# First attention layer: keys and values stored unsplit, dense products by pairs, and another order of TensorE's work in a slot

## The reference

```
q = einsum('bsh,he->bse', x, w_q).reshape(b, sq, GROUPS, HPG, KVC)      # 4 groups of 4 heads, 128 each
k, v = split(einsum('bsh,he->bse', x, w_kv), 2)                         # 4 groups of 128 each
scores = einsum('bqgpd,bkgd->bqgpk', q, k) * KVC ** -0.5
probs = softmax(where(causal, scores, -inf), axis=-1)
ctx = einsum('bqgpk,bkgd->bqgpd', probs, v).reshape(b, sq, HEADS * KVC)
return einsum('bse,eh->bsh', ctx, w_dense)
```

## Time and profile before

| | |
|---|---|
| runs, median | 3868.26 us |
| the profiled execution | 3867.56 us |
| its span, first to last instruction | 3865.7 us |
| TensorE busy, granted clock over the span | 89%, 0.947 |
| VectorE, ScalarE, GpSimd busy | 63%, 41%, 29% |
| stage `l0kv`, first product to the first instruction of `l0h` | 52.4 to 127.3 us |
| heads, first scores to last dense product | 139.4 to 1059 us |

### The profile page before, as it was taken

One profiled execution on the slowest core, in us unless ns is written; L12 is line 12 of the kernel. 1 busy time (PEld: TensorE's weight loads), 2 busy tenths in 40 slices (PEclk: granted clock), 3 DMA queues, 4 the chain that ended last, 5 costly groups with the idle time before them and its releaser, 6 DMA issues. The chain is left out here.

```text
span 3865.7 us, 65600 instructions
## 1 busy us (share of the span) xinstructions
PE 3422.4 (89%) x21360; PEld 2634.4 (68%) x21360; DVE 2453.4 (63%) x4610; ACT 1578.6 (41%) x2855; POOL 1106.9 (29%) x819
## 2 busy tenths in 40 slices
PE   6598998989869799999998669999859999699997
PEld 4477877777747588888886235555438888388883
DVE  4455555655532565666655578889468888388883
ACT  3344444544422444444443224666433333233332
POOL 1000000000013566666664320000013444444444
PEclk8799999999989899999999888999979999899998
DMA  4301000010010100000000232222034443134431
GB/s 144 133 3 45 3 23 24 3 46 1 1 34 0 48 17 18 18 18 18 18 16 0 76 122 80 82 80 83 30 104 115 114 114 97 35 107 114 114 97 48
DMA packets 146336, 216.75 MB, mean 56 GB/s; under 512 B 23824, under 2 KB 87184, under 8 KB 145936
## 3 DMA queue, kind: packets, MB, share of 16 engines
q1 hardware_dynamic: 140112, 207.33, 17.2%
q0 software_dynamic: 6144, 8.39, 1.3%
HBM read 170.45 MB, written 44.96 MB: 56 GB/s over the span
## 5 line engine op out<-in xcount | busy, mean ns | idle before, releaser
L1912 DVE TENSOR_REDUCE l2h_half<-l2h_s 128x1 f32<-128x512 f32 x512 | 337.5, 685 | 49.1 <-PE l2h_s L1814 48.1
L570 DVE TENSOR_REDUCE l0h_negtop<-l0h_sc 128x1 f32<-128x128 f32 (+7 forms) x256 | 192.9, 754 | 224.0 <-PE l0h_sc L485 221.4
L1899 ACT ACTIVATE l2h_PT<-l2h_s 128x1024 f32<-128x1024 f32 x256 | 248.3, 1022 | 163.9 <-PE l2h_s L1824 163.9
L642 ACT ACTIVATE l0h_PTH<-l0h_tp 128x512 fp32r<-128x512 f32 (+3 forms) x384 | 174.6, 488 | 254.8 <-PE l0h_tp L496 254.7
L559 POOL TENSOR_TENSOR l0h_wq_lo<-l0h_wq,l0h_wq_hi 128x256 fp32r<-128x256 f32 x16 | 11.8, 738 | 826.1 <-ACT l0h_wq_hi L628 826.1
L1814 PE MATMUL l2h_s<-l2h_K,l2h_Q 128*128 128x512 f32 x512 | 218.7, 466 | 23.3 <-DMA l2h_K<-l_split 20.8
L496 PE MATMUL l0h_tp<-ident,l0h_probs 128*128 128x128 f32 x1152 | 179.6, 279 | 63.0 <-DVE l0h_PTL L589 62.9
L652 ACT ACTIVATE l0h_probs<-l0h_sc,l0h_negtop 128x128 f32<-128x128 f32 (+7 forms) x256 | 190.3, 744 | 94.3 <-DVE l0h_negtop L570 93.4
L589 DVE TENSOR_TENSOR l0h_PTL<-l0h_tp,l0h_PTH 128x512 fp32r<-128x512 f32 (+3 forms) x384 | 200.8, 550 | 32.2 <-ACT l0h_PTH L642 29.2
L159 POOL TENSOR_TENSOR XN<-XN,n_rstd 128x512 f32<-128x512 f32 x32 | 39.8, 1266 | 594.2 <-DVE n_rstd L140 594.2
L511 PE MATMUL l0h_cx<-l0h_PTH,l0a_VH 128*128 128x256 f32 (+1 forms) x640 | 196.4, 307 | 0.0
(11 more groups left out here) (418 smaller groups left out, 9809.1 us busy)
## 6 DMA issues: line engine op xcount, KB each, us to landing
l3p_decb<-l_decays SPq DMA_DIRECT2D x128, 256.0 KB, 4.4
l3p_w<-L_w SPq DMA_DIRECT2D x34, 512.0 KB, 3.6
l2h_Q<-l_split SPq DMA_DIRECT2D x64, 256.0 KB
l2h_K<-l_split SPq DMA_DIRECT2D x64, 256.0 KB
l3p_prow<-l_decays SPq DMA_DIRECT2D x128, 128.0 KB, 3.1
l_split<-l2q_hi SPq DMA_DIRECT2D x16, 512.0 KB, 3.6
l_split<-l2q_lo SPq DMA_DIRECT2D x16, 512.0 KB, 3.8
l3p_wgu<-L_ffn_w_gate_up SPq DMA_DIRECT2D x32, 256.0 KB, 4.8
```

The lines of the kernel that those rows point to most:

```text
L570: dve.reduce_max(negtop[:, i % 4:i % 4 + 1], sc[s % 2][:, 0:(t + 1) * P], AX_X, negate=True).then_inc(top_ready, 1)
L642: act.activation(PTH[:, pair % 2, 4 * j:4 * j + m, i % 2 * P:(i % 2 + 1) * P], tp[n % 2][:, 0:m * P].rearrange("p (m n) -> p m n", m=m), A ...
L1899: act.activation(PT[:, b, kb, :], s2[kb % 2][:, :], ACT.Exp, scale=L2_SCALE).then_inc(exped, 1)
L1912: dve.reduce_max(half[:, b, t, z:z + 1], bank(slot_of(i))[:, :], AX_X).then_inc(s1_read, 1)
```

## The change

- Keys and values lie in DRAM as they come from the product, in one part. ScalarE and VectorE take every second job and copy it out, and there are eight staging buffers instead of four. Group 0 is loaded after job 23.
- A load goes into the low part's tile (`KL`, `VL`), and GpSimd splits it in place in two passes of 128x1024: the high part is the loaded number plus zero, rounded, and the low part is the difference. SP doesn't wait for landings any more; the semaphores that TensorE waits for come from GpSimd.
- The dense products of a pair are issued together, four slots after its second unit, into both halves of `outp`, and added together. Inverses of row sums are taken by twos.
- High and low queries are made in two halves of 512 columns, and VectorE makes the low queries after the low part of the turn of that slot.
- TensorE's order in a slot becomes: scores or projection, dense pair, values, turn.

```diff
@@ l0_kv @@
-                act.activation(hi[:, n % NB, :], acc[n % 8][:, :], ACT.Copy).then_inc(hi_ready, 1)
-                dve.tensor_tensor(lo[:, n % NB, :], acc[n % 8][:, :], hi[:, n % NB, :].bitcast(F32), ALU.subtract).then_inc(lo_ready, 1)
+                act.activation(raw[:, n % NB, :], acc[n % 8][:, :], ACT.Copy).then_inc(act_kept, 1)
+                dve.tensor_copy(raw[:, n % NB, :], acc[n % 8][:, :]).then_inc(dve_kept, 1)
...
+            def _(pool):
+                pool.wait_ge(zeroed, 1)
+                for b in range(B):
+                    split_keys(pool, kv, 0, b)
+                    split_values(pool, kv, 0, b)
@@ new @@
+def split_keys(pool, kv, g, b):
+    tok = slice(b * S, (b + 1) * S)
+    pool.wait_ge(kv.k_loaded[b], 16 * g + 16)
+    pool.tensor_tensor(kv.KH[:, tok], kv.KL[:, tok].bitcast(F32), kv.zero[:, :], ALU.add).then_inc(kv.k_rounded[b], 1)
+    pool.wait_ge(kv.k_rounded[b], g + 1)
+    pool.tensor_tensor(kv.KL[:, tok], kv.KL[:, tok].bitcast(F32), kv.KH[:, tok].bitcast(F32), ALU.subtract).then_inc(kv.keys_here[b], L0_HPG)
@@ l0_heads, SP and GpSimd: group(g, last) @@
...
-                        keys_arrived(g + 1, 0)
-                        values_arrived(g + 1, 0)
...
+                        for b in range(B):
+                            sp.wait_ge(scores_ready, NU * end + NQ * (b + 1))
+                            load_keys(sp, kd, kv, g + 1, b)
+                            sp.wait_ge(pv_done, NPAIR * end + NPAIR // B * (b + 1))
+                            load_values(sp, vd, kv, g + 1, b)
...
+                    for i in range(L0_HPG):
+                        h = L0_HPG * g + i
+                        if not last or i < L0_HPG - 1:
+                            split_weights(h + 1)
+                    if not last:
+                        for b in range(B):
+                            split_keys(pool, kv, g + 1, b)
+                            split_values(pool, kv, g + 1, b)
@@ l0_heads, TensorE @@
                 def dense(h, i):
-                    pe.wait_ge(ctx_ready, NPAIR * h + i // 2 + 1)
-                        pe.wait_ge(added, NU * h + i)
-                    pe.matmul(outp[:, 0:D], ctxT[:, i // 2 % 2, i % 2 * P:(i % 2 + 1) * P], wd[:, ds(h, 1), :].rearrange("p a n -> p (a n)"),
-                              start=True, stop=True).then_inc(dense_done, 1)
+                    pe.wait_ge(ctx_ready, NPAIR * h + pair + 1)
+                        pe.wait_ge(added, NPAIR * h + pair)
+                    for j in range(2):
+                        mm = pe.matmul(outp[:, j * D:(j + 1) * D], ctxT[:, pair % 2, j * P:(j + 1) * P],
+                                       wd[:, ds(h, 1), :].rearrange("p a n -> p (a n)"), start=True, stop=True)
+                    mm.then_inc(dense_done, 1)
                 def step(h, s):
-                    if u := unit_at(h, s, 2):
-                        turn_probs(*u)
-                    if u := unit_at(h, s, 5):
+                    if (u := unit_at(h, s, 4)) and u[1] % 2:
                         dense(*u)
                     if (u := unit_at(h, s, 3)) and u[1] % 2:
                         weigh_values(*u)
+                    if u := unit_at(h, s, 2):
+                        turn_probs(*u)
@@ l0_heads, VectorE: step @@
-                        elif exists(h + 1 - i):
-                            low_queries(2 * h + (3 if i == 0 else 2), i, sc[s % 2])
                     if u := unit_at(h, s, 2):
-                        invert(*u)
+                        if u[1] % 2:
+                            invert(*u)
                         low_probs(*u)
+                    if kind == "query" and exists(h) and exists(h + 1 - i):
+                        low_queries(2 * h + (3 if i == 0 else 2), i, sc[s % 2])
-                    if u := unit_at(h, s, 5):
+                    if (u := unit_at(h, s, 4)) and u[1] % 2:
                         add_dense(*u)
```

More of the change, by code:

```diff
@@ L275, in l0_kv, with kept @@
         FIRST = TT + NJ
[L277 to L285, removed]
+        def kept(engine, n):
+            engine.wait_ge(dve_kept if n % 2 else act_kept, n // 2 + 1)
         with nc.Block() as block:
@@ L290, in _ @@
             def _(sp):
[L291 to L295, removed]
+                for c in range(DC):
+                    sp.dma_start(wkv[:, c, :], rows(a["L0_attn_w_kv"])[:, c, :]).then_inc(w_loaded, 16)
+                for n, (kind, i, j) in enumerate(jobs):
+                    if n == FIRST + NB // 2:
+                        for m in range(NB):
+                            sp.wait_ge(stored[m], 16 * (FIRST // NB + (m < FIRST % NB)))
                         for b in range(B):
@@ L298, in _ @@
                             load_values(sp, vd, kv, 0, b)
[L299 to L304, removed]
+                    kept(sp, n)
+                    if kind == "k":
+                        sp.dma_start(kd[i][:, j * BANK:(j + 1) * BANK], raw[:, n % NB, :]).then_inc(stored[n % NB], 16)
+                    else:
+                        sp.dma_start(vd.rearrange("g p t n -> p t g n")[:, i], raw[:, n % NB, :].rearrange("p (g n) -> p g n", g=L0_GROUPS)).then_inc(stored[n % NB], 16)
+                for m in range(NB):
+                    sp.wait_ge(stored[m], 16 * (len(jobs) // NB))
             @block.tensor
@@ L322, in _ @@
             def _(act):
-                act.wait_ge(w_loaded, 16)
                 for c in range(DC):
+                    act.wait_ge(w_loaded, 16 * DC)
                     act.activation(w_hi[:, c, :], wkv[:, c, :], ACT.Copy).then_inc(whi_ready, 1)
-                for n in range(len(jobs)):
+                for n in range(0, len(jobs), 2):
                     act.wait_ge(made, n + 1)
-                    wait(act, stored[n % NB], 32 * (n // NB))
-                    act.activation(hi[:, n % NB, :], acc[n % 8][:, :], ACT.Copy).then_inc(hi_ready, 1)
+                    wait(act, stored[n % NB], 16 * (n // NB))
+                    act.activation(raw[:, n % NB, :], acc[n % 8][:, :], ACT.Copy).then_inc(act_kept, 1)
             @block.vector
             def _(dve):
+                dve.memset(kv.zero[:, :], 0.0).then_inc(zeroed, 1)
                 for c in range(DC):
@@ L335, in _ @@
                     dve.tensor_tensor(w_lo[:, c, :], wkv[:, c, :], w_hi[:, c, :].bitcast(F32), ALU.subtract).then_inc(wlo_ready, 1)
-                for n in range(len(jobs)):
-                    dve.wait_ge(hi_ready, n + 1)
-                    wait(dve, stored[n % NB], 32 * (n // NB))
-                    dve.tensor_tensor(lo[:, n % NB, :], acc[n % 8][:, :], hi[:, n % NB, :].bitcast(F32), ALU.subtract).then_inc(lo_ready, 1)
+                for n in range(1, len(jobs), 2):
+                    dve.wait_ge(made, n + 1)
+                    wait(dve, stored[n % NB], 16 * (n // NB))
+                    dve.tensor_copy(raw[:, n % NB, :], acc[n % 8][:, :]).then_inc(dve_kept, 1)
+            @block.gpsimd
+            def _(pool):
[3 more added lines that the diff above has]
+                    split_values(pool, kv, 0, b)
 def l0_heads(nc, k, a, kd, vd, kv):
@@ L545, in _ @@
                     j, c = divmod(n, DC)
[L546 removed]
+                    pe.wait_ge(added, NPAIR * L0_HEADS)
                     wait(pe, x_added, n - 3)
@@ L561, in _, with group @@
                 split_weights(0)
-                with pool.Fori(1, L0_HEADS) as h:
-                    split_weights(h)
+                def group(g, last):
+                    for i in range(L0_HPG):
[6 more added lines that the diff above has]
+                            split_values(pool, kv, g + 1, b)
+                with pool.Fori(0, L0_GROUPS - 1) as g:
+                    group(g, False)
+                group(L0_GROUPS - 1, True)
             @block.vector
@@ L626, in split_weights @@
                     act.wait_ge(wq_loaded, 16 * h + 16)
-                    wait(act, q_made, 2 * h)
+                    wait(act, q_made, 4 * h)
                     act.activation(wq_hi[:, :, :], wq[:, :, :], ACT.Copy).then_inc(whi_ready, 1)
                 def high_queries(n, b, bank):
-                    act.wait_ge(q_made, n)
-                    act.activation(QH[:, b * S:(b + 1) * S], bank[:, :], ACT.Copy, scale=L0_SCALE).then_inc(qh_ready, 1)
+                    for j in range(S // BANK):
+                        act.wait_ge(q_made, 2 * n - 1 + j)
+                        act.activation(QH[:, b * S + j * BANK:b * S + (j + 1) * BANK], bank[:, j * BANK:(j + 1) * BANK], ACT.Copy,
+                                       scale=L0_SCALE).then_inc(qh_ready, 1)
                 def high_probs(h, i):
```

94 lines of the change are left out of this document (44 added, 50 removed).

## The result

| | before | after |
|---|---|---|
| runs, median (us) | 3865.11 (3860.75 to 3872.4) | 3939.86 (3932.48 to 3944.92) |
| span of the profiled execution | 3865.7 | 3943.1 |
| first scores of the heads | 139.4 | 124.4 |
| heads, first scores to last dense product | 919.6 | 1012.8 |

The change makes the kernel slower: the ratio is 1.019 (95%: 1.0164 to 1.0216). The heads take 93.2 us more and begin 15.1 sooner, which makes 78, and the span has 77.4.

A forecast was written before the change was run, and what follows sets the result against it. TensorE was taken to bound the heads, working nearly all the time but waiting for VectorE's low parts and adds. 3867.6 + 96 (heads, with 12 of low clock) - 12 (first stage) = 3951, said as 3950; range 3875 to 3995.

The forecast's parts named there:

- New waits: TensorE in the heads: values wait for low parts, dense pairs for the context copy; 6.45 us a half head with refilling.
- t0: Slot of a half head: values of t2/t3 wait for the low part, with only t0's scores as cover; 1.6 us.
- t2: Slot of a half head: dense pair waits for the copy behind high parts and two half queries; 1.6 us.
- t3: Slot of a half head: values of t6/t7 wait for the first low tile; 1.0 us.
- t1: Slot of a half head: dense pair waits for the copy behind high parts and t0's exponential; 1.1 us.
- t7: Slot of a half head: dense pair waits for the copy behind high parts and t6's exponential; 0.4 us.
- t6: Slot of a half head: values of t4/t5 wait for the low part; 0.35 us.
- W: TensorE's work in one half head, unchanged by the change: 24.9 us, between 24.5 and 25.4.
- Low clock: Heads: time lost to TensorE's lower granted clock, taken as half of before's 14 stretches, 12 us.
- Waits are not hidden: Answers the rival that the heads' new waits are mostly hidden: faster, 3848 with half of 6.45 left; chance 0.10.
- the clock does not fall in every half: Answers the rival that the clock falls in every half head, costing 54 instead of 12: 3992; chance 0.12.
- nothing blocks VectorE: Answers the rival that GpSimd's passes block VectorE in the heads: up to 57 us more, 4007; chance 0.05.

The follow-up runs named there:

- order only: Kernel before with only TensorE's slot order changed (turn last, dense products still single): 4103.67 us, ratio 1.0603.
- Copy first: Kernel after with ScalarE's context copy moved to the front of its step, ahead of high parts and exponential: 3859.14 us, ratio 0.9965.
- values last: Kernel after with the values moved behind the turn on TensorE, the dense pair staying ahead of it: 3850.4 us, ratio 0.9957.
- turn first: Kernel after with TensorE's turn moved back ahead of the dense pair and the values: 3766.31 us, ratio 0.9732.
- unsplit only: Kernel before with only the unsplit keys and values (first stage, loads, GpSimd's splits): 3860.5 us, ratio 0.9973.
- low queries only: Kernel before with only VectorE's low queries moved behind the low part of that slot's turn: 3823.11 us, ratio 0.9887.

## Why the prediction was right

The forecast of 3950 came out 10 above the median, by its own mechanism.

- *Waits that go.* The turn's wait for low parts and the dense product's wait for adds vanish, as said. The single edits tell the two apart. For the turn's wait of 62.9 the moved order suffices ("order only" leaves 1.0), and so nearly do the late low queries (4.7 left). The wait for adds is taken by the pairs; the moved order alone raises it from 19.1 to 184.7.
- *New waits.* Values for low parts and dense pairs for the copy, longest in t0 and t2. With the 0.2 that the list leaves out, slot by slot: t2 1.6 (1.6 said), t3 1.0 (1.0), t0 1.6 (1.6), t1 1.14 (1.1), t7 0.36 (0.4), and t6, at 533.13 in the next half, 0.43 (0.35); together 6.1 (6.05). PE's idle time in the heads comes to 159.6 + 186 x 0.2 = 197 by the same reckoning (200 said). Copy first and values last take the two kinds apart.
- *Work.* W was 24.9; "turn first" has (838.7 - 2)/32 = 26.15 a half without low clock and two waits of together 1.18 listed and 0.2 unlisted each, so W is some 24.6. The half of after, (1012.8 - 27)/32 = 30.8, leaves 6.2 for new waits (6.45 said). Together they are 0.55 below the forecast of 31.35, which is 17 us less. The 0.07 for refilling the array behind each wait, 0.4 a half in the sum, is shown by no run: in the kernel after the first product of the values is followed by the second after 0.22 us behind a wait (484.16) and after 0.20 without one (502.10), 0.02 at that place.
- *Low clock.* 12 us were said, half of before's, as no wait would be longer than 1.85; one was, of 1.98 in the last half. Low clock cost 27, in 9 stretches instead of 14, seven of them twice as long. The profiled execution is the longest of four (3944.92), so the usual loss may be some us less. This step was mis-sized by 15 us and nearly cancels the 17: that the total came so close is in part luck. Here are 10 us of one in the kernel after (windows as in the earlier trace rows):

```profile
494.00:496.00 2.00, 2.00 (x14) 2.00 (x14) 0.00 (x0) 0.25 (x1) 0.00 (x0) 0.63 0.00 0
496.00:498.00 2.00, 1.42 (x6) 1.05 (x6) 1.29 (x4) 1.13 (x5) 0.00 (x0) 0.50 0.00 0
498.00:500.00 2.00, 2.00 (x9) 1.62 (x8) 0.00 (x0) 0.00 (x0) 0.00 (x0) 0.50 0.00 0
500.00:502.00 2.00, 2.00 (x9) 1.66 (x8) 1.14 (x3) 1.32 (x4) 0.00 (x0) 0.67 0.00 0
502.00:504.00 2.00, 2.00 (x19) 1.94 (x18) 1.67 (x3) 0.00 (x0) 0.00 (x0) 1.00 0.00 0
```

- *First stage.* GpSimd begins at 93.49 (93.5 said), its passes take 2.34 to 2.40 as the earlier trace rows had them, and the stage gives 14.2 instead of 12. GpSimd does bind, some 9 us behind the last store.
- *GpSimd beside VectorE.* No cost, 686 against 687 ns, and "unsplit only" has the heads as long as before. The rule that was weighed there (the Trainium skill, SBUF — State Buffer, "Who interferes with whom") agrees with these rows.
- *The rivals.* Waits are not hidden (6.2 a half against the 3.8 from which that rival decided); the clock does not fall in every half (9 stretches); nothing blocks VectorE.

Two expectations in the experiments failed clearly, on sizes that the same walk would have given: order only (adds behind low queries) and values last (the copy behind queries, the pair as cover).

## What to carry to other kernels

When engines work in order through a round trip (turn, high part, low part, product), the work between a producer and its consumer is the cover: walk each round trip in the new order before moving a step, and put the step that starts the chain first. A pair of edits can each hand its wait to the other, so test them together as well as singly; and an edit that gains under one order may be worth nothing under another. Split a loss into listed waits, low clock and the rest before explaining it.

## What had not been expected of the hardware

Low clock did not follow the length of a wait alone. In the kernel after, no listed wait on PE near the stretch that begins at 494.5 is longer than 1.41 us, and it lasts twice as long as before's (some 6.8 us against 3.4). Four stretches begin 126 us apart (494.5, 620.8, 747.1, 873.4), which is two heads, while the half that follows the first, with waits of 1.49, 0.81 and 1.50 at the places of 1.40, 0.81 and 1.41, has none.

Still, the falls follow the longer waits. In the kernel after each of the nine stretches begins 1.0 to 1.5 us behind the end of a wait of 1.4 us or more, though the heads have some 60 of these. In "turn first", "low queries only" and "values last" no wait between the first scores and the last half head is longer than 1.2 us, and there the clock falls only behind the first scores; in "low queries only" that is one stretch left of 14, though only a third of the listed waits had gone. Why the clock falls behind one such wait and not behind the next stays open; no run here was made for it.
